# q and k as two float32r parts, two heads side by side in TensorE's row halves, k resident per sequence, and query 0 attending inside the projection

## What is computed

```python
dist = jnp.abs(idx[:, None] - idx[None, :])
attend = (dist <= 128) | (idx < 1)[:, None] | (idx < 1)[None, :]
def attn(x):                                   # x: [4, 2048, 256]
    q, k, v = x @ Wq.T, x @ Wk.T, x @ Wv.T     # split into 16 heads of 16
    logits = where(attend, q k^T / 4, -inf)
    return softmax(logits) v @ Wo.T
def ffn(x):
    h = bitlinear(x, w_fc) + gate * (x @ v.T @ fast_b.T @ u.T)
    return bitlinear(relu(h) ** 2, w_proj)     # ternary weights times a row's mean size
x = x + attn(layernorm(x)); x = x + ffn(layernorm(x))
```

## Time and profile before

| | |
|---|---|
| runs | 1388.05 us median of 3 (1383.82 to 1388.18) |
| profiled execution: span | 1385.3 us (first to last instruction; the profile gives no other time for it) |
| PE busy | 1241.6 us, 90% |
| DVE busy | 1057.3 us, 76% |
| ACT, POOL busy | 801.1 us, 777.9 us |
| projection | 0 to 181 us |
| attention | 181 to 906 us |
| query 0 and weights | 906 to 965 us |
| feed | 965 to 1385 us |

### The profile page before, as it was taken

The page is one execution under the profiler, slowest core; times in us unless marked ns, Lnnn a source line. Parts: engine busy times, 40 slices in busy tenths (PEclk is TensorE's granted clock), DMA queues, the critical chain, the costliest instruction groups (busy, mean ns, idle before and its releaser), DMA issues. The chain is left out here.

```text
span 1385.3 us, 34119 instructions
## 1 busy us (share of the span) xinstructions
PE 1241.6 (90%) x10205; PEld 827.8 (60%) x10205; DVE 1057.3 (76%) x3288; ACT 801.1 (58%) x1404; POOL 777.9 (56%) x1337
## 2 busy tenths in 40 slices
PE   5999939999999989999899999745799999999997
PEld 4888814445444444444444445322688888888886
DVE  6999758888888878888788888262667767677674
ACT  4778805666766757666577676611345445454454
POOL 1445564777777767777677778820134334334343
PEclk9999957999999999999999999968799999999999
DMA  3999999656687556875468753385212112121100
GB/s 123 333 337 331 309 197 151 104 113 122 117 140 137 102 109 118 137 137 104 105 117 141 137 104 86 138 288 175 91 47 90 48 48 88 45 82 54 45 32 31
DMA packets 174564, 180.61 MB, mean 130 GB/s; under 512 B 24612, under 2 KB 169016, under 8 KB 173368
## 3 DMA queue, kind: packets, MB, share of 16 engines
q1 hardware_dynamic: 174392, 178.57, 54.0%
HBM read 118.47 MB, written 59.25 MB: 128 GB/s over the span
## 5 line engine op out<-in xcount | busy, mean ns | idle before, releaser
L923 DVE CUSTOM_DVE_ANT_0 a_masked<-a_turn,a_band 128x385 f32<-128x385 f32 (+1 forms) x1024 | 512.1, 539 | 91.3 <-PE a_turn L789 72.3
L873 ACT ACTIVATE a_weights<-a_score 128x1024 f32<-128x1024 f32 x384 | 391.8, 1025 | 133.6 <-PE a_score L807 132.1
L682 POOL TENSOR_SCALAR_AFFINE_SELECT a_weights<-a_weights 128x256 f32<-128x256 f32 (+1 forms) x768 | 351.2, 496 | 122.1 <-ACT a_weights L873 122.1
L1338 POOL TENSOR_TENSOR f_square<-f_relu 128x512 f32<-128x512 f32 x128 | 150.9, 1183 | 313.7 <-ACT f_relu L1434 312.8
L830 PE MATMUL a_sum<-a_weights,a_v 128*17 128x384 f32 (+2 forms) x2816 | 228.8, 399 | 3.4 <-POOL a_weights L682 3.3
L1434 ACT ACTIVATE f_relu<-f_bank 128x512 f32<-128x512 f32 x128 | 76.7, 599 | 186.5 <-PE f_bank L200 183.4
L786 PE MATMUL a_turn<-a_k,a_q 96*128 96x384 bf16 (+1 forms) x512 | 165.6, 328 | 11.8 <-issue 6.6
L1466 DVE TENSOR_TENSOR f_square_lo<-f_square,f_square_hi 128x512 fp32r<-128x512 f32 x128 | 106.4, 842 | 89.1 <-POOL f_square L1338 89.1
L1410 PE MATMUL f_bank<-w_w_t,f_square_hi 128*128 128x256 f32 x512 | 133.2, 293 | 16.4 <-DVE f_square_lo L1466 15.1
L807 PE MATMUL a_score<-a_q,a_k 99*128 99x384 bf16 (+2 forms) x704 | 129.1, 275 | 3.0 <-ACT a_weights L873 3.0
L279 POOL TENSOR_TENSOR p_parts<-p_rest,p_parts 128x512 bf16<-128x512 f32 x64 | 74.1, 1169 | 97.8 <-ACT p_parts L342 97.8
(11 more groups left out here) (184 smaller groups left out, 2592.1 us busy)
## 6 DMA issues: line engine op xcount, KB each, us to landing
qk_parts<-p_parts SPq DMA_DIRECT2D x64, 384.0 KB, 3.2
a_q<-qk_parts SPq DMA_DIRECT2D x48, 192.0 KB, 5.0
a_q<-qk_parts SPq DMA_DIRECT2D x144, 64.0 KB, 4.8
v_ones<-p_va SPq DMA_DIRECT2D x16, 544.0 KB, 5.0
p_x<-in_x SPq DMA_DIRECT2D x16, 512.0 KB, 6.0
k_whole<-p_kf SPq DMA_DIRECT2D x16, 512.0 KB, 3.7
attention<-a_o SPq DMA_DIRECT2D x16, 512.0 KB, 3.3
f_o<-attention SPq DMA_DIRECT2D x16, 512.0 KB, 4.3
```

Of the source, the lines that this page charges most:

```text
L682: ins = pool.affine_select(out=cut, in_=cut, compare_op=ALU.is_ge, fill=0.0, base=0, pattern=[[0, NQ // 2], [0, m], [sign, P]], channel_mu ...
L873: act.activation(pe_w[:, us.upar, c * CHUNK:(c + 1) * CHUNK], score[c % 2][:], ACT.Exp).then_inc(s_exp, 1)
L923: dve.tensor_tensor_reduce(out=masked[:, j, first:3 * P + 1], in0=bank[:, lo:hi + 1], in1=band[:, lo:hi + 1], scale=1.0, scalar=NEG, op0=A ...
L1338: pool.tensor_tensor(r2[:, j % 4, :], r[:, j % 4, :], r[:, j % 4, :], ALU.mult).then_inc(s_sq, 1)
```

## The change

q and k are kept as two float32r parts (HIGH and LOW) in float32 instead of three in bfloat16. Three slots of 16 rows (instead of six) make a product, so a head takes 48 rows, 50 with two shift rows, and two heads lie in partitions 0 and 64 on: each pair of heads is multiplied by two instructions that name different row halves and write different banks. Key 0 lies in a gap of two columns behind every block of 128 keys (pitch 130), written by POOL in the projection, so a maxima tile is one product of 390 columns. k is loaded once for each sequence, by chunks of 512 tokens. The lags shrink to 2, 3, 4, 5, 6, 7. The order on PE is by pairs of tiles, and M moves from turn 3 to turn 4. MID is gone, and the cuts are two for each pair of heads. Query 0's scores are 16 more columns of v's product, from weights made in the projection's beginning, and its softmax and sums stand at the projection's end. The stage of query 0 keeps only the weights.

```diff
 def stage_project(...):
+            sp.dma_start(x0[:], x[:, 0:1, :].rearrange("b a d -> (b a) d")).then_inc(s_x0, DMA)
...
     pool:
-                        pool.wait_ge(s_mid, q.g * 4 + u + 1)
-                        pool.tensor_tensor(parts[:, q.par, u, PLACE[u // KT][LOW], :], rest[:, u, :], ...
+                        pool.tensor_tensor(keys[:, :, :, P:KPITCH], first, one[:]..., ALU.mult).then_inc(s_gap, 1)
     tensor:
+            pe.wait_ge(s_x0v, 9)
+            for k in range(KT):
+                ins = pe.transpose(x0_bank[:, k * B:(k + 1) * B], x0n[:, k * P:k * P + P], ident[0:B, 0:B])
...
+            pe.wait_ge(s_x0v, 12)
+            for k in range(KT):
+                for m in range(KT):
+                    ins = pe.matmul(c_bank[:, k * B * H:(k + 1) * B * H], w_in[:, 1, m, k * P:k * P + P],
+                                    q0_d[:, m].rearrange("p b h -> p (b h)"), start=(m == 0), stop=(m == KT - 1))
...
+                    for t in range(TB):
+                        wait(pe, s_vout, q.g * TB + t - 1)
+                        three_pass(pe, v_bank[t % 2][:, 0:D + H], [a[:, cut] for a in xh], [a[:, cut] for a in xl],
+                                   wv(wv_hi, q), wv(wv_lo, q)).then_inc(s_v, 1)
...
             sweep(pe, body, LP)
+            pe.wait_ge(s_rv, 1)
+            pe.transpose(turn_bank[0:B * H, 0:P], m_tok[:], ident[:]).then_inc(s_rpe, 1)
+            pe.wait_ge(s_rv, 3)
+            pe.matmul(over_bank[:, 0:B * H], ones[0:B * H, :], m_diag[:], start=True, stop=True).then_inc(s_rpe, 1)
+            pe.wait_ge(s_rexp, 1)
+            for n in range(NB):
+                for b in range(B):
+                    ins = pe.matmul(sum_bank[QR * b:QR * b + H, 0:VROW], w0[:, b, n, :], v_of[:, b, n, 0:VROW],
+                                    start=(n == 0), stop=(n == NB - 1))
...
     scalar:
+            act.activation(wq_t[:].rearrange("p k n -> p (k n)"), banks[0][:], ACT.Copy).then_inc(s_whi, 1)
...
+            act.wait_ge(s_x0v, 3)
+            act.activation(x0_sd[:], x0_ve[:], ACT.Sqrt).then_inc(s_x0sd, 1)
...
     vector:
+            dve.wait_ge(s_x0, DMA)
+            dve.bn_stats(x0_stats[:], x0[:]).then_inc(s_x0v, 1)
...
+            for w in range(2):
+                dve.wait_ge(s_whi, w + 2)
+                for k in range(KT):
+                    ins = dve.tensor_tensor(wt_lo[:, w, k]..., ALU.subtract)
...
+            for b in range(B):
+                ins = dve.tensor_tensor(wv_lo[:, b, :, 0:D], banks[2][:].rearrange("p (k n) -> p k n", k=KT),
+                                        wv_hi[:, b, :, 0:D].bitcast(F32), ALU.subtract)
...
 attention:
-TURN_OF_M, TURN_OF_S, TURN_BANKS = 3, TILES + 1, 3
+TURN_OF_M, TURN_OF_S, TURN_BANKS = 4, TILES + 1, 3
-L_KEY0, L_MAX, L_SHIFT, L_SCORE, L_SUM, L_OUT, L_STORE = 2, 3, 4, 6, 7, 8, 9
+L_MAX, L_SHIFT, L_SCORE, L_SUM, L_OUT, L_STORE = 2, 3, 4, 5, 6, 7
+AFTER_PAIR = (
+    (("score", 0),), (("score", 1), ("M", 0)), (("sum", 0),), (("score", 2), ("sum", 1)),
+    (("sum", 2),), (("score", 3), ("sum", 3)), (("score", 4), ("sum", 4)),
+    (("score", 5), ("sum", 5), ("S", 0)))
+SUM_ORDER = (1, -1, 2, 4, 0, 3)
     sync, a unit's loads:
+                    for half in range(2):
+                        r0, h0 = half * HEAD_ROWS, (u.hq * 2 + half) * HD
+                        r1, r2 = r0 + PARTS * HD, r0 + SLOT_ROWS
+                        for c in CHUNKS_OF[u.gi]:                      # ((0, 1), (2,), (3,), ())
...
+                            sp.dma_start(dst[r0:r1], src.rearrange("r s f t -> (r s) f t")).then_inc(landed, DMA)
+                            sp.dma_start(dst[r1:r2], src[:, PLACE[1][HIGH]]).then_inc(landed, DMA)
...
+                        sp.dma_start(dst[r0:r1], src.rearrange("r s f t -> (r s) f t")).then_inc(landed, DMA)
+                        sp.dma_start(dst[r1:r2], src[:, PLACE[0][HIGH]]).then_inc(landed, DMA)
...
+                    sp.wait_ge(s_shift, u.n + 1)
+                    for half in range(2):
+                        for part in range(SHIFT_ROWS):
...
                 if (u := at(L_STORE)) and u.hq == UPG - 1:
                     sp.wait_ge(s_o, u.n + 1)
     gpsimd:
+            def cut_heads(u, f):
+                exp_turn.wait(u.n * CHUNKS + (f + 1) * CHUNKS // 2)
+                w = pe_w[:, u.upar].rearrange("p (f c q) -> p f c q", f=PAIRS, q=P)
+                for first, sign in ((CUT_AHEAD, 1), (CUT_BEHIND, -1)):
+                    cut = w[:, f, first::CUT_STEP, :]
...
     tensor:
+                def max_pair(i):
...
+                    for j in (2 * i, 2 * i + 1):
+                        bank_read(TURN_OF_TILE[j])
+                    for j in (2 * i, 2 * i + 1):
+                        half, f, t, _ = head_of_tile(j)
...
+                        pe.matmul(turn[TURN_OF_TILE[j] % TURN_BANKS][:, lo:hi],
+                                  qw[ux.gpar][ux.hq][r0:r0 + SLOT_ROWS, f, t * P:t * P + P],
+                                  kt[ux.hq][r0:r0 + SLOT_ROWS, f, k0 + lo:k0 + hi],
+                                  start=True, stop=True).then_inc(s_tile, 1)
+                def score_chunk(c):
...
+                    for _, col, kb, qb, m in tiles:
+                        k0 = (us.gi * TB + kb) * KPITCH
+                        for half in range(2):
+                            r0 = half * HEAD_ROWS
+                            ins = pe.matmul(
+                                score[c % 2][:, half * GT + col * P:half * GT + (col + m) * P],
+                                kt[us.hq][r0:r0 + rows, f, k0:k0 + P],
+                                qw[us.gpar][us.hq][r0:r0 + rows, f, qb * P:(qb + m) * P], start=True, stop=True)
...
 query 0:
-def stage_row_zero(nc, qk_dram, kf_dram, va_dram, o_dram, w_proj, ahead, weights):
+def stage_weights(nc, ahead, weights):
```

## The result

The changed kernel takes 1679.22 us (median of 4 runs, 1663.81 to 1687.97), the kernel before 1388.12 (4 runs, 1383.82 to 1388.46): a ratio of 1.2107, 95% interval 1.2041 to 1.2172. The forecast was 1328 us, range 1290 to 1396; it was wrong, and on the wrong side. The profiled execution has a span of 1679.9 us against 1385.3.

A forecast was written before the change was run, and what follows sets the result against it. Attention sets the time, TensorE slightly longer than VectorE's 8.8 us floor. 1385.3 + 8.8 + 2.6 + 9.4 - 5 - 51 - 0.6 - 24.4 = 1325, with the median 2.7 above: 1328 us, range 1290 to 1396.

The forecast's parts named there:

- Rival (4): Attention: TensorE's clock falls to 1.2 GHz, about +190 us, 1570 in total; chance 0.05.
- PE's 13.5 a unit at 1.2 GHz: Attention: TensorE's own work per unit, 7.5 us at full clock, becomes 13.5 if the clock falls.
- "Together": Attention: two row-half products run at once, 0.17 us a pair of tiles and 0.24 a score chunk.
- rivals (1) to (3): Attention's halves: together, 1328 us (chance 0.50); weight loads in one line, 1363 (0.25); not side by side, 1395 (0.13).
- The full unit, 9.53 by hand: Attention: hand schedule of one full unit, 9.53 us; edge units 9.0, mean 9.27, before SyncE's stalls.
- gaining 51: Attention: 64 units at 9.7 us instead of 10.5 save 51 us.
- data reach DVE 0.38 after issue: Attention: latency in the hand schedule from TensorE issuing a pair of tiles to VectorE reading it, 0.38 us.
- The M bubble: Attention: turned maxima take one of three banks, so the next pair waits and VectorE loses 0.44 us a unit.
- SyncE's stalls: Attention: late shift-row DMAs stall score chunks up to 4.0 us, about 0.4 us a unit.
- 7.7 us a sequence: Attention: SyncE's stalls summed over a sequence, which the prediction turned into 0.4 us a unit.
- The norm of group 0: Projection's beginning: VectorE's first norm starts at 19.8 us instead of 11.01, behind query-0 weight steps; +8.8 us.
- +9.4 of the projection's tail: Projection's end: query 0's softmax and sums run after v, ending at 190.5 instead of 181.25; +9.4 us.

The follow-up runs named there:

- e2: Changed kernel, but each maxima and score product takes 112 or 114 rows at full height, the two heads summed; q and k cleared first: 1543.6 us.
- e3: Changed kernel, but both products of each pair, maxima and scores, use the same row half, so they run one after the other: 1942.4 us.
- e6: Changed kernel with all 64 rows of each half named in maxima and score products, q and k cleared first: 1512.7 us.
- e13: Probe without the layer: TensorE's units with 48 and 50 rows, 64 rows, or the old bf16 products, from 2.4 GHz, one long pause a unit; no kernel time.
- e9: Probe without the layer: units of changed and old kernels, started at 1.2 or 2.4 GHz, with or without waits for VectorE; no kernel time.
- e1: Probe without the layer: TensorE alone runs blocks of its own products without waits, each starting at 2.4 GHz; paired halves took 0.179 us a pair.
- (b) of e1: Block of 160 single 48-row float32r products, all in one row half, without waits: busy 40.00 of 40 us at a grant of 0.50.
- (a) of e9: Block of the changed kernel's unit, 48 and 50 rows in halves, no waits, started at 1.2 GHz: back at 2.4 GHz only after 55 us.
- e4: Changed kernel, but VectorE takes each maximum over 130 of the window's 388 columns only: 1554.6 us.
- e7: Changed kernel with each pair of maxima products issued twice into the same banks, 48 rows kept: 1714.3 us.
- e11: Changed kernel with maxima only over the query's own block and key 0, tiles of 130 columns instead of 388: 1585.2 us.
- e10: Changed kernel with 64 rows of each half named in score products only, maxima kept at 48, q and k cleared first: 1607.9 us.

## Why the prediction was wrong

- **Rival (4), the clock falls.** This is what happened, 1679 us with a grant of 0.55 in attention, and I gave it 0.05 and 1570. The reason against it was the step that failed: "in attention the grant is 0.98, and no wait that the change adds is longer than a few us". It read the grant of the old kernel as a property of the stage, though the change halves the rows that every maxima and score product names (96 and 99 become 48 and 50), and e2, e3 and e6 show that the grant hangs on them. And it took waits of "a few us" for short: with these rows one of 1.25 us sufficed (e13), and in the kernel itself two of some 0.6 and 0.8 us close together. The row that should have given it weight was in hand, the grant of 0.75 in the query-0 stage with TensorE busy 33.23 of 57 us. The price was too low as well: PE's 13.5 a unit at 1.2 GHz is 14.9 dense (e9) and 15.8 in the kernel's units at 1.2 GHz.
- **Cause.** Shown: at 1.2 GHz the 48-row unit can be busy without a gap and not get 2.4 GHz back for 55 us (e9), 64 named rows repair most of it without a product more (e6), one pause brings it down (e13). The kernel starts attention down already, after the stage boundary, as the one before did: by the clock records it stood at 1.2 GHz from 203 to 272 us, the one before from 175 to 223, which then stayed up (0.98 from 220 to 880). The Trainium skill, TensorE: Matmul & The Clock Gate, section What's actually happening, has the gate follow how busy TensorE has been, with the warm-up a matter of time and not of how many products; blocks (b) of e1 and (a) of e9, busy throughout at 0.50, speak against that for products in few rows, and the measurement decides. The falls come behind the clump at the turned maxima (11 of 14), and where that is gone (e4), behind the stalls for the shift rows; no run takes both away, and none says what the clock would then do. Not settled either is how rows and the length of products work together. Rows are not all: with 48 rows, maxima made twice have a grant of 0.68 (e7), maxima a third as wide 0.50 (e11).
- **"Together", the question of rivals (1) to (3).** Right: 0.179 us a pair in e1, 0.29 with what follows in the kernel, where e2, with two products one after the other, has 0.46 (701.38 to 701.84). But the sizes were short: in the dense unit a pair before a chunk costs 0.24 to 0.28, not 0.17, a chunk 0.24 to 0.39, and the unit 8.6 instead of 7.5.
- **The full unit, 9.53 by hand.** This is a second step that failed, apart from the clock. At 2.4 GHz it is 10.98 (mean of five in e10) and an edge unit 10.55 (mean of four) instead of 9.0: 10.8 on average, where the kernel before takes 10.49. So even with the clock up attention would have lost some 18 us instead of gaining 51, and the time would have been about 1385.3 + 20.8 - 23.6 + 18 = 1400, just above the range: an estimate from these units. The term at fault is "data reach DVE 0.38 after issue": it is 0.60 for these pairs (479.12 to 479.72), and with three banks a pair can be issued only when the first tile of the last is read. A step is 0.49 + 0.14 + 0.60 = 1.23 us, where VectorE's two tiles are 0.97. With the old kernel's single tiles, one could be made while another was read. The M bubble came as forecast, somewhat larger (VectorE waits 0.66 before the tile at 474.80, against 0.44), and VectorE's tail shrank unforeseen: den, d0 and rden take 0.18, 0.18 and 0.24, where den alone took 0.56.
- **SyncE's stalls.** Right in size: scores waiting for shift rows cost 0.41 a unit and 4.3 us at most in e2, whose unit is longer than the one forecast. In the changed kernel there is one, of 6.1 us. What the sum left out is that such a stall also takes the clock: a fall follows that one, and six of e4's nine falls stand behind one. (The prediction's own 7.7 us a sequence of 16 units are 0.48 a unit, not 0.4; it moves the sum by 5 us.)
- **Projection and query 0.** The norm of group 0 starts at 18.77, forecast 19.8; attention's first load at 202.05, forecast 202; the stage of the weights is 23.6 us shorter, forecast 24.4 (of the +9.4 of the projection's tail, 190.5 less 181.25 gives only 9.25); the first exponential comes at 245.66 instead of 234, at half clock.

## What to carry to other kernels

Before products are made lower to run side by side, ask what holds TensorE's clock: write down the rows that its products name and its longest waits, and give "the clock falls" a real chance and the price of the whole stage at 1.2 GHz, whatever the grant is now. Look at the granted clock first in the profile after; a TensorE that is 90% busy may be slow rather than loaded. When two tiles become one step on few banks, price the step as read plus signal plus latency, not as the longer of two engines.

## What the runs showed of the hardware

- The clock has memory: the same 48-row unit stood at 1.00 for 95 us when it started at 2.4 GHz, with eight waits a unit, and at 0.50 for 136 us when it started at 1.2 GHz, with four (e9).
- Rows that hold only zeros count as rows: 64 named instead of 50 in the scores alone took the grant from 0.56 to 0.72 (e10); 64 in the maxima too, 0.89 (e6).
- Single 48-row products back to back, busy without a gap, lost 2.4 GHz (0.50 for 40 us), while the same products in two halves at once kept it for 19 us (e1).
- In the kernels with 48 rows the clock also fell behind two waits of some 0.6 and 0.8 us within 2 us (11 of 14 falls of the changed kernel), while eight waits of 0.2 us spread over the unit left it up (e9).
- One pause of 1.25 us took 2.4 GHz from the 48-row unit both times that it met it there, from the 64-row unit once in five and for 3.4 us, from the 96-row unit not in five (e13).
